# Two delta-attention layers: row factors in place of normalised keys and queries, and a new order around the triangular solve

## The reference, cut to what matters

```python
q = l2norm(silu((x @ Wq).reshape(b, t, H, DK)))   # l2norm: x * rsqrt(sum(x*x) + 1e-6)
k = l2norm(silu((x @ Wk).reshape(b, t, H, DK)))
v = silu((x @ Wv).reshape(b, t, H, DV))
beta = sigmoid(x @ Wb) * 2.0
def step(S, inps):
    qi, ki, vi, bi = inps
    pred = einsum('bhkv,bhk->bhv', S, ki)
    S = S + bi * ki[..., :, None] * (vi - pred)[..., None, :]
    return (S, einsum('bhkv,bhk->bhv', S, qi))
o = rmsnorm(scan(step), onorm_w) @ Wo
```

## Time and profile before

| | |
|---|---|
| Median of 3 runs | 326.36 us (326.19 to 326.78) |
| The profiled execution, its own time | 325.2 us |
| Its span in the trace | 323.4 us |
| TensorE busy | 277.4 us, 86% |
| DVE busy | 205.5 us, 64% |
| ScalarE busy | 100.9 us, 31% |
| GpSimd busy | 35.7 us, 11% |
| DMA | 18.70 MB, 58 GB/s over the span |
| Mean granted TensorE clock | 0.925 of full |

### The profile page before, as it was taken

How to read it: one execution, slowest core, us unless ns; L and a number is a source line. 1 busy time by engine, 2 the same in 40 slices (tenths; PEclk the granted TensorE clock), 3 DMA queues, 4 the chain that set the end, 5 groups by cost and what they waited for, 6 DMA issues and landing times.

```text
span 323.4 us, 9623 instructions
## 1 busy us (share of the span) xinstructions
PE 277.4 (86%) x4361; PEld 209.4 (65%) x4361; DVE 205.5 (64%) x398; ACT 100.9 (31%) x205; POOL 35.7 (11%) x32
## 2 busy tenths in 40 slices
PE   0999999999798999949799998975889999579865
PEld 0566677788787976628786764745877676445443
DVE  4248879969856658755673488673662255288991
ACT  1023311220010137871225433676222442341210
POOL 2961100210780012000000000000000000000000
PEclk9999999999999999975978999996796999769989
DMA  7999500000000000000001206000000000000001
GB/s 300 425 416 430 251 1 0 2 0 0 2 0 0 3 1 2 0 4 2 0 4 44 90 0 244 34 0 4 2 3 2 2 0 0 0 2 1 0 0 41
DMA packets 2729, 18.70 MB, mean 58 GB/s; under 512 B 464, under 2 KB 784, under 8 KB 1936
## 3 DMA queue, kind: packets, MB, share of 16 engines
q1 hardware_dynamic: 2704, 18.34, 14.3%
HBM read 18.01 MB, written 0.33 MB: 57 GB/s over the span
## 4 chain that ended last, share of the span: by engine, by line
PE 64%; DVE 21%; ACT 10%; issue 3%; DMA 1%; ACTq 0%; DVEq 0%
PE ps L1143 13%; PE ps L1438 11%; PE ps L1187 4%; PE ps L1520 3%; PE ps L1647 3%; PE ps L1511 3%; PE ps L1201 2%; PE ps L1610 2%; PE ps L1530 2%; PE ps L1133 2%; ACT wl L497 2%; PE ps L1559 2%; DVE big L1011 2%; PE ps L1576 2%; DVE wt L1008 2%
## 5 line engine op out<-in xcount | busy, mean ns | idle before, releaser
L1143 PE MATMUL ps<-big,cwb 128*128 128x384 f32 x120 | 42.7, 509 | 8.0 <-DVE cwb L663 8.0
L1143 PEld LDWEIGHTS ps<-big,cwb 128*128 128x128 f32 x120 | 23.5, 199 | 22.7 <-DVE cwb L663 8.0
L1511 PE MATMUL ps<-wt,big 32*32 32x32 f32 x1280 | 16.7, 209 | 10.0 <-DVE wt L986 5.4
L1438 PE MATMUL ps<-xT,wl 128*128 128x320 f32 x88 | 24.5, 434 | 0.7 <-ACT wguT L364 0.5
L1511 PEld LDWEIGHTS ps<-wt,big 32*32 32x32 f32 x1280 | 14.7, 121 | 12.1 <-DVE wt L986 6.1
L283 POOL TENSOR_TENSOR xs<-xs,big 128x640 f32<-128x640 f32 x14 | 21.5, 1535 | 1.4
L1438 PEld LDWEIGHTS ps<-xT,wl 128*128 128x128 f32 x88 | 16.6, 190 | 7.8 <-ACT wguT L364 0.7
L1008 DVE COPY_PREDICATED wt<-cst,ps 128x320 f32<-128x320 int32 x16 | 8.1, 503 | 19.6 <-PE ps L1520 19.6
L340 ACT COPY pecT<-ps 128x384 f32<-128x384 f32 x12 | 5.7, 478 | 43.5 <-PE ps L1143 43.5
L1520 PE MATMUL ps<-wt,big 32*32 32x32 f32 x1280 | 15.9, 212 | 3.1 <-ACT wt L505 2.4
L1201 PE MATMUL ps<-wt,pecT 128*128 128x256 f32 x72 | 16.6, 381 | 1.4 <-DVE big L759 1.4
(11 more groups left out here) (275 smaller groups left out, 532.4 us busy)
## 6 DMA issues: line engine op xcount, KB each, us to landing
big<-in_patches SPq DMA_DIRECT2D x6, 960.0 KB, 11.2
wl<-in_layers SPq DMA_DIRECT2D x2, 2176.0 KB, 20.2
wf<-in_ffn SPq DMA_DIRECT2D x1, 2112.0 KB, 16.7
wl<-in_layers SPq DMA_DIRECT2D x2, 1040.0 KB, 16.0
wt<-in_tok SPq DMA_DIRECT2D x1, 1536.0 KB, 23.6
wt<-in_tok SPq DMA_DIRECT2D x1, 768.0 KB, 8.5
cwb<-in_conv SPq DMA_DIRECT2D x1, 640.0 KB, 3.9
cst<-in_constants SPq DMA_DIRECT2D x1, 320.0 KB, 23.9
```

The source lines that it names most:

```text
L1143: last = mm(ps[:, i % 4, 0:GRP], cwc[:, k, c * P:(c + 1) * P], xg[:, g, k, :], start=(k == 0), stop=(k == KC - 1))
L1438: last = mm(ps[:, bank, 0:NT], w(c, j), x[:, c, :], start=(c == 0), stop=(c == CH - 1))
L1511: last = mm(ps[r, 4 + b, 32 * k:32 * k + 32], apm[r, NB * b + k, own], tc_[r, NB * b + k, :], start=True, stop=True)
```

## The change: what it does

- K and Q are no longer normalised. The small products take the SiLU outputs `skq` as they are. The key half of their result is multiplied, row by row, by `negc` = (1 + tanh) / -(sum k^2 + eps); the query half by `bm`, the causal mask scaled by `negc` (20 ScalarE copies of 64 columns a layer). V is scaled by `sr` = (sum k^2 + eps)^(1/2). The query's norm is an eps term in the output norm: its squares (scaled by `(DH*eps)^(1/2)`) are summed by `blk` into the banks that the output's squares are then added to.
- Beta is a small product with 8 columns (`betas`), the keys' squares another with 4 columns (`key_squares`).
- The small products run in one pass: group `pj` 4 into banks 4 to 7, the others into banks 0 to 3. V follows them instead of preceding them.
- Two of the four table loads ahead of the levels go. The `wg` scaling moves from ScalarE, ahead of the levels, to DVE, behind the solve.
- Of the FP4 weights, piece 2 is finished in the seam; piece 3 and part of piece 5 move behind the solve.
- In the seam the patches' part of K is computed beside the class token, the patches' `m0` ahead of it, and the patches' final norm (`rsx`) is made early. The `h0` sum moves from GpSimd to DVE in layer 1. The `keep_clock` products of the small-product phase (3), of the seam (2 and 2) are left out. In the cut diff, `weights(p, 0..3)` are the four quantising parts of piece p; `cols` is the class columns in layer 0 and all columns in layer 1.

```diff
@@ scalar, layer @@
-                for a in range(2):
+                silu_kq(0)
+                nc.scalar.activation(kqsq[:, 0], skq[:, 0], ACT.Square).then_inc(S["silu"], 1)
+                silu_kq(1)
+                nc.scalar.activation(tb, ps[:, 5, 0:NG], ACT.Tanh, scale=0.5).then_inc(S["silu"], 1)
+                nc.scalar.copy(apm[:, 16:NG, :], ps[:, 4:8, 0:P]).then_inc(S["p5"], 1)
+                causal(0, 8)
+                nc.scalar.activation(vs[:, 8:NG, :].rearrange("p g d -> p (g d)"), ps[:, 6, 0:3 * P], ACT.Silu
+                y_out(1, 0)
+                nc.scalar.activation(vs[:, 0:8, :].rearrange("p g d -> p (g d)"), ps[:, 7, 0:C], ACT.Silu
+                causal(8, 12)
+                y_out(1, 1)
                 nc.scalar.preload_act_table_set("natural_log_exp_and_others")
-                    rsqrt(act_, rkq[:, a], ps[:, 1 + 2 * a:3 + 2 * a, 0:NT], "rkq", EPS_RMS, k=2 * a + 1, layer=l)
-                nc.scalar.preload_act_table_set("silu_and_others")
...
-                nc.scalar.preload_act_table_set("natural_log_exp_and_others")
-                for c in range(CH):
-                    nc.scalar.activation(wg[:, c, :], wg[:, c, :], ACT.Copy,
-                                         scale=vec[:, V_N2 + 2 * l + c:V_N2 + 2 * l + c + 1]).then_inc(S["wgs"], 1)
+                y_out(2, 0)
+                nc.scalar.activation(sr, nsse, ACT.Ln, scale=-1.0).then_inc(S["sr"], 1)
+                y_out(2, 1)
+                nc.scalar.activation(sr, sr, ACT.Exp, scale=0.5).then_inc(S["sr"], 1)
+                causal(12, NG)
+                y_out(3, 0)
+                y_out(3, 1)
+                nc.scalar.activation(kqsq[:, 1], skq[:, 1], ACT.Square, scale=(DH * EPS_RMS) ** 0.5)
+                y_out(4, 0)
+                y_out(4, 1)
@@ vector, layer @@
-                for part_ in range(4 if l else 2):
-                    weights(3 + 2 * l, part_)
-                v.tensor_tensor(kh[:, :, :], skq[:, 0], rkq[:, 0], ALU.mult).then_inc(S["kq"], 1)
-                v.scalar_tensor_tensor(kbq[:, 0], bt[:, :, :], 1.0, kh[:, :, :], ALU.add, ALU.mult)
-                v.tensor_tensor(kbq[:, 1], skq[:, 1], rkq[:, 1], ALU.mult).then_inc(S["kq"], 1)
+                dve.wait_ge(S["ss_mm"], EACH["ss_mm"] * l + 1)
+                v.tensor_scalar(nsse, ps[:, 0, 0:NG], EPS_RMS, -1.0, ALU.add, ALU.mult).then_inc(S["ss"], 1)
+                step(v.reciprocal(nrec, nsse))
+                v.scalar_tensor_tensor(negc, tb, 1.0, nrec, ALU.add, ALU.mult).then_inc(S["c"], 1)
...
+                dve.wait_ge(S["ap_mm"], EACH["ap_mm"] * l + 2)
+                keys_scaled(0, 3)
+                pairs(0)
+                keys_scaled(3, 1)
+                keys_scaled(4, 1)
+                pairs(1)
...
-                        if lev == 2:
-                            v.tensor_tensor(apm[:, g, 64:P], apm[:, g, 64:P],
-                                            map_[:, 64:P].unsqueeze(1).broadcast_to([P, NB, 64]), ALU.mult
-                                            ).then_inc(S["pm"], 1)
+                    if lev == 1:
+                        queries_scaled(0, 3).then_inc(S["pm"], 1)
+                    if lev == 2:
+                        queries_scaled(3, 1)
+                        queries_scaled(4, 1).then_inc(S["pm"], 1)
+                    if lev == 3:
+                        v.tensor_tensor(bv[:, :, :], vs[:, :, :], sr.unsqueeze(2).broadcast_to([P, NG, DH]), ALU.mult
...
+                for c in range(CH):
+                    v.tensor_scalar(wg[:, c, :], wg[:, c, :], vec[:, V_N2 + 2 * l + c:V_N2 + 2 * l + c + 1], None, ALU.mult
+                                    ).then_inc(S["wgs"], 1)
-                    weights(3, 2)
+                    weights(3, 0)
+                else:
+                    weights(5, 2)
                 for j in range(CH):
                     v.scalar_tensor_tensor(oT[:, j, :], ps[:, 6 + j, 0:NT], onw, ro[:, j, :], ALU.mult, ALU.mult)
-                    weights(3, 3)
+                    weights(3, 1)
+                else:
+                    weights(5, 3)
                 for j in range(CH):
-                    v.tensor_tensor(xT[:, j, :], xT[:, j, :], ps[:, 2 + j, 0:NT], ALU.add).then_inc(S["x"], 1)
+                    v.tensor_tensor(xT[:, j, :], xT[:, j, :], ps[:, 4 + j, 0:NT], ALU.add).then_inc(S["x"], 1)
+                if l == 0:
+                    weights(3, 2)
+                    weights(3, 3)
+                else:
+                    v.tensor_tensor(hT0[:, :, :], hT0[:, :, :], m0[:, :].unsqueeze(1).broadcast_to([P, CH, NT]), ALU.add
+                                    ).then_inc(S["h0"], 1)
@@ tensor, seam and layer @@
-            keep_clock(4, 2)
+            for c in range(CH):
+                mm(ps[:, 0, 0:NW], wmean[:, 1, c:c + 1].broadcast_to([P, P]), lc[:, 0, c, :],
+                   start=(c == 0), stop=(c == CH - 1))
...
+            project_cols(1, L_K, 0, patches)
             norm_sum(ps[:, 5, NW:NT], sqx[:, :, NW:NT], ones[:, :]).then_inc(S["x_var"], 1)
-            keep_clock(4, 2)
+            project_cols(2, L_K, 1, patches)
...
+                for j in range(CH):
+                    last = project_cols(1 + j, L_K, j, cols)
+                for j in range(CH):
+                    last = project_cols(3 + j, L_Q, j, slice(0, NT))
+                if l:
+                    key_squares()
+                    betas()
+                else:
+                    betas()
+                    key_squares()
...
+                pe.wait_ge(S["silu"], EACH["silu"] * l + 4)
+                per_window(4).then_inc(S["ap_mm"], 1)
+                pe.wait_ge(S["ss"], EACH["ss"] * l + 1)
+                for pj in range(4):
+                    last = per_window(pj)
+                last.then_inc(S["ap_mm"], 1)
+                pe.wait_ge(S["p5"], EACH["p5"] * l + 1)
+                for c in range(CH):
+                    mm(ps[:, 6, 0:C], hT[:, c, P:2 * P], wvb[:, c, :, 0:P], start=(c == 0), stop=(c == CH - 1))
...
+                pe.wait_ge(S["pm"], EACH["pm"] * (l + 1))
+                for j in range(CH):
+                    mm(ps[:, 2 + j, 0:NT], blk, kqsq[:, 1, j, :], start=True, stop=False)
...
-                    mm(ps[:, 4 + j, 0:NT], blk, osq[:, j, :], start=True, stop=True)
+                    mm(ps[:, 2 + j, 0:NT], blk, osq[:, j, :], start=False, stop=True)
```

More of the change, by code:

```diff
@@ L205, in build @@
         wd = lw(L_D, C, FC)
[L208 removed]
+        once = """sqsum cw vecs consts tokw tokw2 ffnw cwc ones conv copied squared xsum part redc redq var_mm rsr
             vec_mm vmean cls_v cls_mm cls_n kqb_mm kqb vb_mm vbias wkvg wqg q_mm q k_mm1 k_free stat_mm rk softmax score
@@ new lines, in silu_kq, with causal, y_out @@
+                    nc.scalar.activation(skq[:, a], ps[:, bank:bank + 2, 0:NT], ACT.Silu).then_inc(S["silu"], 1)
+                def causal(first, end):
+                    for g in range(first, end):
+                        last = nc.scalar.activation(bm[:, g, :], map_[:, 64:P], ACT.Copy, scale=negc[:, g:g + 1])
+                    last.then_inc(S["bm"], 1)
+                def y_out(lev, b):
+                    act_.wait_ge(S["y_mm"], EACH["y_mm"] * l + 2 * (lev - 1) + b + 1)
+                    if lev > 1:
+                        act_.wait_ge(S["z_mm"], EACH["z_mm"] * l + 2 * (lev - 2) + b + 1)
+                    nc.scalar.copy(yc[:, NB * b:NB * (b + 1), :], bank32(4 + b, slice(0, P))).then_inc(S["y"], 1)
@@ L651, in weights @@
                     quant_near(src)
+                elif part == "sum":
+                    quant_near(src, ops=1)
+                elif part == "difference":
+                    quant_near(src, ops=2)
                 else:
@@ new lines, in key_squares @@
+                def key_squares():
+                    pe.wait_ge(S["silu"], EACH["silu"] * l + 2)
+                    for pj in range(4):
+                        p = pj // 2
+                        mm(ps[:, 0, HP * pj:HP * pj + HP], kqsq[:, 0, pj % 2, P * p:P * p + P], heads, start=True, stop=True)
+                    for a in range(2):
+                        last = mm(ps[64 * a:64 * a + 64, 0, 4 * HP:5 * HP], kqsq[:, 0, a, NW:NT], heads, start=True, stop=True)
+                    last.then_inc(S["ss_mm"], 1)
@@ L1504, in layer, with level_z @@
+                def level_z(b):
+                    pe.wait_ge(S["y"], b + 1)
+                    for k in range(NB):
+                        for q in range(4):
+                            r = slice(32 * q, 32 * q + 32)
+                            last = mm(ps[r, 6 + b, 32 * k:32 * k + 32], ttc[r, NB * b + k, :],
+                                      yc[r, NB * b + k, :], start=True, stop=True)
+                    last.then_inc(S["z_mm"], 1)
                 with pe.Fori(0, LEVELS - 1):
```

275 lines of the change are left out of this document (126 added, 149 removed).

## The result

| | before | after |
|---|---|---|
| Median of the runs on one chip | 326.57 us (326.19 to 328.48) | 316.72 us (315.18 to 317.4) |
| Profiled execution, its span | 325.2, 323.4 us | 315.18, 313.4 us |
| Mean granted clock | 0.925 | 0.939 |
| Layer 0: first Y, end of the first Z | 140.26, 148.1 | 133.13, 140.96 |
| Layer 0: Z of level 4, solve, `oT`, sum into `xT` | 159.15, 161.28, 172.38, 175.15 | 151.18, 154.24, 165.44, 168.94 |

The ratio is 0.9716 (0.9672 to 0.9759): the changed kernel is 10 us faster, where 16.4 were forecast, and its 316.7 lies 0.2 outside the range. The table already tells where the difference lies: layer 0 reaches its first Y 7.1 us earlier, as forecast.

A forecast was written before the change was run, and what follows sets the result against it. Bound: a chain alternating between engines, TensorE 64%, DVE 21%, ScalarE 10%. Terms -10.5 + 0.9 (layer 0) - 9.6 (layer 1) + 1.6 + 1.2 = -16.4 from 325.2 gave 308.8, plus 1.16 gave 309.9, rounded to 309.8; range 305 to 316.5.

The forecast's parts named there:

- the seam: Layer 0 only, from the class projection to the K activation: 0.9 us gained.
- Up to the first Y: Layer 0, K through betas, key squares and small products: first Y at 133.3 against 140.26.
- Between `oT` and the sum: Layer 0, output norm to sum into `xT`: `quant_step` replaces `quant_back`, 0.9 us lost, once.
- The query squares: Ahead of the solve: four passes of 320 columns, 1.1 us, half hidden by an old gap, 0.6 lost.
- the first correction, instruction supply: First pass of the level loop: TensorE waits for instructions, 0 to 2 us a layer, taken as 0.8, 1.6 in all.
- The clock, second correction: Levels of each layer: TensorE's clock may fall, 0 to 0.85 us a level, taken as 0.6 a layer, 1.2 in all.
- three cycles and 0.2: First Z to Z of level 4: three cycles of 3.73 us, plus 0.2 for mask copies delaying a Y copy.
- ScalarE queue: Rival: small ScalarE steps queue ahead of the Y copies, +6 us a layer, 322; chance 0.04.
- DVE becomes the bound: Rival: behind the solve, `wg` at 2.9 us makes `oT` wait, about 1.5 us a layer, 313; chance 0.08.
- No fall and no supply stall: Rival: V products keep the clock up and DVE's waits cover the fetches, 307; chance 0.16.
- The loop is fetched again in each pass: Rival: levels 2 to 4 each wait for their instructions, 16 us a layer, 342; chance 0.02.
- The clock stays low throughout: Rival: low clock through levels and solve in both layers, 4.2 us a layer, not 0.6, 317; chance 0.09.

The follow-up runs named there:

- the pads alone: Changed kernel with 16, 32, 48 or 64 idle 32x32 products at program start: 312.58, 311.12, 315.8 and 318.03 us.
- run 2: Changed kernel with the `wg` scaling put back on ScalarE ahead of the first Y copy: 318.99 us, ratio 0.9786 to the kernel before.
- run 7: Changed kernel with 32 idle products at program start, `weights(3, 1)` behind layer 0's sum, and filler products around the final norm: 308.29 us.
- pad 40: Changed kernel with 40 idle products at program start and `weights(3, 1)` behind layer 0's sum: 311.42 us, ratio 0.9541 to the kernel before.
- pad 16: Changed kernel with 16 idle 32x32 products at program start: 312.58 us, ratio 0.9549 to the kernel before.
- pad 32: Changed kernel with 32 idle 32x32 products at program start: 311.12 us, ratio 0.9518 to the kernel before.
- first version of run 6: Changed kernel with 32 idle products at program start and `weights(3, 1)` moved behind layer 0's sum: 307.78 us, ratio 0.9406 to the kernel before.

## Why the prediction was wrong, step by step

**Up to the first Y it held.** First Y 133.13 (forecast 133.3), second half 135.41 (135.7), K's activation 124.29 (124.5), so the seam gave 1.1 for 0.9. Betas and key squares took 0.79 + 0.34 + 0.99 + 0.21 = 2.3 in the chain (2.2). Eight mask copies took 2.00, 0.25 each, under the bound of 0.31. `wg` on DVE took 1.82 for two (1.9), with DVE still idle 1.18 and 1.15 ahead of `oT`:

```profile
160.75 1.82 DVE L1068 TENSOR_SCALAR wl<-wl,vec 128x1408 f32<-128x1408 f32 x2
...
165.44 0.55 DVE L1077 SCALAR_TENSOR_TENSOR big<-ps,vec,wt 128x320 f32<-128x320 f32 x1 [1.18 <-ACT wt L309]
...
168.94 0.88 DVE L1085 TENSOR_TENSOR xT<-xT,ps 128x320 f32<-128x320 f32 x2
```

Between `oT` and the sum layer 0 lost 0.7 (3.50 us against 2.77), and DVE held it, as forecast at 0.9. The query squares took 1.31 (1.1). (The forecast's last addition, 308.8 + 1.16, is 309.96 and not 309.9, which changes nothing.)

**The step that failed is the first correction, instruction supply at 0.8 us a layer (0 to 2).** I saw 0.68 and 0.32 us of "issue" in the earlier trace rows and its layer 0 twin and took them for the whole price, with ScalarE's `wg` as a cover beside it. They were only what the cover left visible. The right reading was at hand: in both layers Z ended 7.8 and 8.4 us after the first Y, and the forecast had 4.9 (133.3 to 136.6 + 1.57). I had no row that showed the 640 instructions going through faster on their first pass, and should have bounded the stretch by the whole 7.8, not by the stall. In its place: stalls of 0.57 + 2.27 + 0.30 = 3.1 us in layer 0 and 0.58 + 2.15 = 2.7 in layer 1. The solve of layer 0 started 7.0 us earlier than before, where 10.5 - 0.8 - 0.6 = 9.1 was forecast; layer 1 by itself gained 12.35 - 6.21 = 6.1, where it was 9.6 - 1.4 = 8.2. So 2.1 us a layer are missing, and 0.3 of each are the query squares (the way from Z of level 4 to the solve grew by 0.9, not 0.6); the other 1.8 are this step, net of what else moved: the term was too small by 2.3 and 1.9, the first Y came 0.2 and 0.3 earlier than forecast, and the rest is clock.

**The clock, second correction (0.6 a layer),** was roughly right in size. From the end of the first Z to that of level 4 are 11.8 us in layer 0 and 11.35 in layer 1, against three cycles and 0.2, 11.4; 0.3 of the 11.8 are the last stall. In layer 1 the cost lies in the first pass instead: its 8.4 us are 3.5 more than 4.9, and the stalls are 2.7 of that. That makes about 0.2 and 0.7 for the clock, an estimate by difference. In layer 0 the clock fell behind the 2.27 us stall and came back after 3.4 us. In layer 1 it fell at 210.1, during Z's products and ahead of the 2.15 us stall, and came back at 216.9. Windows of 1 us, layer 0 and then layer 1:

```profile
139.00:140.00 1.00, 0.00 (x0) 0.00 (x0) 0.00 (x0) 0.00 (x0) 0.00 (x0) 1.00 0.00 0
...
142.00:143.00 1.00, 1.00 (x92) 1.00 (x87) 0.91 (x2) 0.49 (x2) 0.00 (x0) 0.50 0.00 0
...
146.00:147.00 1.00, 0.95 (x111) 0.83 (x98) 0.96 (x4) 0.32 (x2) 0.00 (x0) 1.00 0.00 0
...
210.00:211.00 1.00, 1.00 (x100) 1.00 (x93) 0.00 (x0) 0.89 (x2) 0.00 (x0) 0.55 0.08 16
```

What I had left out is the clock behind the solve of layer 1. There 12.35 us of lead shrank to 10.0. Two places, each a product that does the same work as before:

```profile
238.14 1.92 PE L1330 MATMUL ps<-cst,wf 128*128 128x128 f32 x8
239.84 2.80 PE L1668 MATMUL ps<-big,wl 128*128 128x320 f32 x8
...
278.61 6.55 PE L1733 MATMUL ps<-wguT,pecT 128*128 128x352 f32 x16 [0.46 <-ACT pecT L548]
```

Before, these took 1.23, 2.32 and 5.00 us. The first two are 1.1 of the loss (`oT` to the sum 3.85 against 2.73), the third 1.5. Over the fourteen profiled kernels the time from that sum to the end has three values, 68.4 to 68.5, 69.7 to 69.8 and 70.7 to 71.4 us; in the last the first gate and up products take 6.5 to 6.7, in the others 5.0. Where the low clock makes these products slow, the time is 70.7 or more; what parts 69.7 from 68.4 wasn't followed. It doesn't go with what an edit does there, since nothing of that stretch differs: the pads alone give 68.4 (16), 71.4 (32), 69.7 (48) and 71.3 (64). The parts, 2.1 + 2.1 + 2.35, less 0.1 that layer 0's sum did better than forecast, are the 6.4 that are missing. That the second part comes from the earlier, different rhythm of the small products is only argued; the filler didn't settle it, and it stays open.

**The rivals.** "ScalarE queue" (322) fell with the changed kernel's own trace, where the first two Y copies start 0.04 and 0.06 us after their Y ends (134.06 and 137.13 in layer 0), and with run 2. "DVE becomes the bound" (313) fell too: `oT` was released by ScalarE, with DVE idle 1.18 and 1.15 us ahead of it. "No fall and no supply stall" (307) had neither of its two conditions. "The loop is fetched again in each pass" (342) is wrong for this kernel: the cycle from Z of level 3 to Z of level 4 is 3.73 us, before and after, and the transfers are as many as the blocks with the loop counted once. "The clock stays low throughout" (317) gives nearly the measured time by another way: in layer 0 the clock was low for 3.4 of the 16 us from the first Z to the query squares. A right total is no evidence for a mechanism.

**The rules.** "TensorE: Matmul & The Clock Gate", Part 1, of the Trainium skill says that sustained activity releases the fast level. The fall behind the 2.27 us stall fits it, and so does the one in layer 1 at 210.1, behind idle times of 1.40 and 0.58 us. So does the fall at 272 in run 7, behind eight microseconds in which TensorE was busy for only 3.24, as far as one execution goes. "Runtime: NRT & Kernel Launch", Instruction fetch mechanics, of the Trainium skill warns of a taken branch out of the window. No run here shows that case: the jump back of this loop brought no further transfer. What cost time was straight code, small products that outrun the next block, at 2.7 to 3.1 us a layer.

## What to carry to other kernels

An "issue" gap inside a run of products that wait for nothing was supply here: count instructions (four to a small float32 product) between such gaps, and look for a 16 KB transfer behind each. Before crediting the removal of a wait, ask what the same stretch would take if that wait were gone, and bound it by the time from its first to its last instruction, not by the stall that is left beside the wait. Where a first pass of many small instructions is on the path, the place of the block borders is worth microseconds: here 32 idle products at the start of the program brought 316.7 to 311.1, and with one quantising step moved 307.8, of which a part is clock that neither edit was shown to cause.

## What the runs showed of the hardware

- A TensorE block is 256 instructions (16 KB), sent for when the block ahead of it is entered. From the end of one stall to the end of the next, within one pass of the loop, 3.45 to 4.15 us pass (pad 40, layer 1; run 2, layer 1). Where the entry has to be placed by the count of passes, it is 3.0 to 3.7 (estimates; pad 16 and pad 32). The visible transfer is over 2.3 to 2.5 us ahead of the first instruction that runs again (134.2 to 136.74, 138.0 to 140.34); what fills that time is not shown. 256 instructions of 32x32 passes need 1.3 to 1.5 us at the high clock, an estimate from 1.57 and 1.83 us for 160 passes.
- A block seems to be entered when the engine's list gets to it, even if its first instruction waits for a semaphore. With pad 32 (first version of run 6, layer 0) the border lies at the second Y, which waited for DVE from 133.4 to 134.81, and the block after it was there at 136.94: 3.5 us after 133.4, but only 2.1 after 134.81, less than in any other run.
- Once through, a body of 640 instructions is held: later passes show no such wait, and 19 transfers serve 8762 TensorE instructions. With a border at its end, the step to the second pass cost 2.99 us, once.
- The clock's falls lie in other places from one profiled kernel to the next, also where the kernels differ only by a pad; the same 16 products cost 5.0 or 6.5 to 6.7 us for it. The executions of the changed kernel and its variants scatter by 1 to 9 us each; how much of that is the clock, one profiled execution of each doesn't show.
